# Attention values and output projections dealt as one step per PSUM bank, with one bias addition per bank of values

## The reference

```python
x = x + _L0_xattn_ref(_layernorm(x), ctx_512, ...)
x = x + _L0_ffn_ref(_layernorm(x), ...)
x = x + _L1_xattn_ref(_layernorm(x), ctx_512, ctx_512, ...)
x = x + _L1_ffn_ref(_layernorm(x), ...)
...
# layer 0 attention: causal self-attention plus attention to the context
v = _heads(x @ Wv + bv)
y = jnp.einsum('bhqk,bhkd->bhqd', jax.nn.softmax(att, axis=-1), v)
...
vc = _heads(cross_input @ Wcv + bcv)
y = y + jnp.einsum('bhqk,bhkd->bhqd', jax.nn.softmax(attc, axis=-1), vc)
return y.transpose(0, 2, 1, 3).reshape(x.shape[0], T, C) @ Wp + bp
```

## Time and profile before

| | us |
|---|---|
| median of three runs | 2109.8 |
| lowest and highest run | 2107.66, 2111.73 |
| the profiled execution, its time | 2102.05 |
| its span in the trace | 2100.2 |
| TensorE busy | 1729.6 (82%) |
| VectorE busy | 1344.1 (64%) |
| ScalarE busy | 1165.2 (55%) |
| GpSimd busy | 740.4 (35%) |
| mean granted clock of TensorE | 0.912 |

### The profile page before, as it was taken

One profiled execution on the slowest core, in us unless ns is written; L12 is line 12 of the kernel. 1 busy time (PEld: TensorE's weight loads), 2 busy tenths in 40 slices (PEclk: granted clock), 3 DMA queues, 4 the chain that ended last, 5 costly groups with the idle time before them and its releaser, 6 DMA issues.

```text
span 2100.2 us, 34206 instructions
## 1 busy us (share of the span) xinstructions
PE 1729.6 (82%) x10016; PEld 745.4 (35%) x10016; DVE 1344.1 (64%) x2478; ACT 1165.2 (55%) x2178; POOL 740.4 (35%) x984
## 2 busy tenths in 40 slices
PE   5676688898889879997889778987989888777776
PEld 1233234432344324433443234422443244232224
DVE  6454575667656575767566665757576766717378
ACT  1353347555855566554855575555755485571586
POOL 3303323632254325431353324431453223241034
PEclk7788889999999989998999989998999999986988
DMA  7213321323132312322132313231142213005023
GB/s 193 66 51 91 93 74 35 106 69 101 38 89 78 89 51 62 102 77 77 42 107 72 103 31 87 77 98 51 44 104 68 80 47 87 21 16 166 22 80 101
DMA packets 106991, 159.96 MB, mean 76 GB/s; under 512 B 20656, under 2 KB 83248, under 8 KB 106800
## 3 DMA queue, kind: packets, MB, share of 16 engines
q1 hardware_dynamic: 101904, 156.43, 26.8%
q10 hardware_dynamic: 4896, 1.18, 0.3%
HBM read 105.00 MB, written 51.38 MB: 74 GB/s over the span
## 4 chain that ended last, share of the span: by engine, by line
PE 49%; DVE 14%; POOL 13%; issue 11%; ACT 8%; DMA 4%; SPq 2%; ACTq 0%; POOLq 0%; DVEq 0%
PE acc L1375 11%; PE mx L1340 11%; PE st L1361 9%; DVE nmax L1161 6%; PE misc L1315 4%; PE misc L1287 4%; POOL qk L810 3%; PE misc L1327 3%; PE misc L1402 3%; POOL parts L812 2%; POOL parts L808 2%; PE misc L1429 2%; POOL parts L814 2%; ACT probs L918 1%; DMA hid<-in_L_ffn_w_dram 1%
## 5 line engine op out<-in xcount | busy, mean ns | idle before, releaser
L1161 DVE TENSOR_REDUCE nmax<-mx 128x1 f32<-128x512 f32 (+2 forms) x1376 | 877.9, 673 | 471.2 <-PE mx L1340 280.3
L918 ACT ACTIVATE probs<-st 128x512 f32<-128x512 f32 (+3 forms) x1536 | 772.0, 549 | 592.2 <-PE st L1361 393.9
L1340 PE MATMUL mx<-stack 96*128 96x512 bf16 (+3 forms) x1536 | 570.5, 383 | 189.7 <-DVE nmax L1161 136.0
L1361 PE MATMUL st<-stack 99*128 99x512 bf16 (+3 forms) x1536 | 566.0, 377 | 63.4 <-ACT probs L918 51.7
L1340 PEld LDWEIGHTS mx<-stack 96*128 96x128 bf16 x1536 | 154.0, 100 | 414.2 <-DVE nmax L1161 307.4
L1361 PEld LDWEIGHTS st<-stack 99*128 99x128 bf16 x1536 | 151.4, 100 | 414.1 <-ACT probs L918 250.2
L808 POOL TENSOR_TENSOR parts<-qk,zero 128x512 bf16<-128x512 f32 x94 | 98.2, 1045 | 304.5 <-ACT qk L901 304.5
L820 POOL TENSOR_TENSOR nparts<-nmax,zero 128x16 bf16<-128x16 f32 x96 | 20.7, 215 | 398.9 <-DVE nmax L1161 392.2
L1375 PE MATMUL acc<-probs,v_x 128*32 128x512 f32 x1024 | 154.3, 678 | 0.0
L1375 PE MATMUL acc<-probs,v_f 128*32 128x512 f32 x1024 | 142.2, 629 | 0.4 <-ACT probs L918 0.3
L1364 PE MATMUL st<-mask_st,identb 128*128 128x128 bf16 x512 | 112.5, 222 | 0.0
(11 more groups left out here) (235 smaller groups left out, 2044.0 us busy)
## 6 DMA issues: line engine op xcount, KB each, us to landing
parts_xk<-parts SPq DMA_DIRECT2D x48, 128.0 KB
parts_xq<-parts SPq DMA_DIRECT2D x48, 128.0 KB
stack<-parts_xq SPq DMA_DIRECT2D x32, 192.0 KB, 3.2
stack<-parts_xk SPq DMA_DIRECT2D x32, 192.0 KB, 3.6
...
```

Source lines behind the costliest of these rows:

```text
L918: act.activation(probs[:, j % P_SLOTS, c, T - w:], st_bank(n, 4 * j + c)[:, 0:w], ACT.Exp, scale=SCALE).then_inc(exp_done, 1)
L1161: dve.tensor_reduce(nmax[:, ring, first:first + NT * (len(cs) - 1) + 1:NT], src, AX.X, ALU.max, negate=True).then_inc(mx_free, 1)
L1340: last = pe.matmul(o, stack[0:ROWS, r, 0, c, P * i:P * i + P], stack[0:ROWS, r, 1, c, 0:w], start=True, stop=not causal)
L1361: last = pe.matmul(o[:, 0:w], stack[0:AUG, r, 1, c, P * j:P * j + P], stack[0:AUG, r, 0, c, T - w:T], start=True, stop=not causal)
```

## The change

`v` and `residual` become two steps each, with an index h of the bank, and the hand-written lists give each half its own entry, followed by an empty place. VectorE adds the bias of a whole bank of values in one 128x512 instruction (before, two of 128x256). The semaphore `v_done` goes: `values` waits for the reads of both `misc` banks. In the last turn's ends, where no slots are (`AFTER`), the halves follow each other directly. The waits of `stats` and of the tail's loads name the halves; nothing else is changed there.

```diff
--- before.py
+++ after.py
@@ -169,12 +169,16 @@
             [("stack", u) for u in us[2 * m:3][:2]]]
 
 
+def values_of(b, p):
+    return [("v", b, p, 0), None, ("v", b, p, 1), None]
+
+
 def project(b, p):
-    return [("v", b, p), None] + project_qk(b, p)
+    return values_of(b, p) + project_qk(b, p)
 
 
 def layer0_end(b):
-    return [("mid_bias", b), ("y_T", b, "A"), None, None, ("residual", b, "A"), None]
+    return [("mid_bias", b), ("y_T", b, "A"), None, None, ("residual", b, "A", 0), None, ("residual", b, "A", 1), None]
 
 
 def layer0_ffn(b):
@@ -196,7 +200,7 @@
 
 
 def layer1_end(b):
-    return [("y_T", b, "C"), None, ("residual", b, "C"), None, ("stats", b, "E"), None, None, ("norm", b, "E"),
+    return [("y_T", b, "C"), None, ("residual", b, "C", 0), None, ("residual", b, "C", 1), None, ("stats", b, "E"), None, None, ("norm", b, "E"),
             ("finish", b), None, None]
 
 
@@ -211,11 +215,11 @@
     if b == 0:
         return [("load0", 1)] + slots(us[:1], project(0, "s"), 1, True) + slots(us[1:3], weights([0, 1]), 1) + \
             slots(us[3:4], tokens0(1), 1) + slots(us[4:5], project_qk(1, "x"), 1) + \
-            slots(us[5:8], [("v", 1, "x"), ("load_mid", 0)] + weights([2, 3]) + project_qk(1, "s"), 1)
+            slots(us[5:8], values_of(1, "x") + [("load_mid", 0)] + weights([2, 3]) + project_qk(1, "s"), 1)
     more = b + 1 < B
     loads = [("load1", b - 1)] + ([("load0", b + 1)] if more else [])
     if b == 1:
-        start = slots(us[:1], [None] * 6 + layer0_end(0) + [("v", 1, "s")], 2) + \
+        start = slots(us[:1], [None] * 6 + layer0_end(0) + values_of(1, "s"), 2) + \
             slots(us[1:5], layer0_ffn(0) + layer1_start(0), 2)
     else:
         start = slots(us[:5], [None] * 6 + layer1_end(b - 2) + layer0_ffn(b - 1) + layer1_start(b - 1), b + more)
@@ -232,9 +236,9 @@
 
 
 FIRST = turn_units(0)
-BEFORE = [("load0", 0), ("consts_load", 0)] + tokens0(0) + [("consts", 0)] + first_qk(0, "x", FIRST) + [("v", 0, "x")] + \
+BEFORE = [("load0", 0), ("consts_load", 0)] + tokens0(0) + [("consts", 0)] + first_qk(0, "x", FIRST) + values_of(0, "x") + \
     warm_up(FIRST)[3:] + [("consts_rest", 0)]
-AFTER = close((B - 2, "f", NU - 1)) + warm_up(turn_units(B))[:3] + layer1_end(B - 2) + [("v", B - 1, "f")] + \
+AFTER = close((B - 2, "f", NU - 1)) + warm_up(turn_units(B))[:3] + layer1_end(B - 2) + values_of(B - 1, "f") + \
     warm_up(turn_units(B))[3:] + slots(turn_units(B), [], B, True) + close((B - 1, "f", NU - 1)) + layer1_end(B - 1)
 
 TURNS = [[s for s in steps if s] for steps in
@@ -242,8 +246,8 @@
 
 
 RING_USES = {
-    "misc": {"weights": 1, "ctx_T": 1, "norm_T": 2, "project": 1, "v": 2, "negmax_T": 1, "heads_out": 1,
-             "y_T": 2, "residual": 2, "quant_T": 2, "hidden": 1, "down_T": 1, "down": 1},
+    "misc": {"weights": 1, "ctx_T": 1, "norm_T": 2, "project": 1, "v": 1, "negmax_T": 1, "heads_out": 1,
+             "y_T": 2, "residual": 1, "quant_T": 2, "hidden": 1, "down_T": 1, "down": 1},
     "parts": {"project": 1},
 }
 
...
@@ -1139,15 +1142,13 @@
                                          ALU.add).then_inc(misc_free[slot], 1)
 
             def v(s):
-                p = s.args[0]
-                bias = Bv[p + "v"][:, :].rearrange("p (h d) -> p h d", d=D)
-                for k in range(2):
-                    wait_misc_full(dve, s, k)
-                    slot = misc_slot(s, k)
-                    for t in range(2):
-                        dve.tensor_tensor(v_aug[p][:, 2 * k + t, :, 0:D],
-                                          misc[slot][:, C * t:C * t + C].rearrange("p (h d) -> p h d", d=D), bias,
-                                          ALU.add).then_inc(*((v_done[p], 1) if t == 0 else (misc_free[slot], 1)))
+                p, h = s.args
+                bias = Bv[p + "v"][:, :].rearrange("p (h d) -> p h d", d=D).unsqueeze(1).to_broadcast([P, 2, H, D])
+                wait_misc_full(dve, s)
+                slot = misc_slot(s)
+                dve.tensor_tensor(v_aug[p][:, 2 * h:2 * h + 2, :, 0:D],
+                                  misc[slot].rearrange("p (t h d) -> p t h d", t=2, d=D), bias,
+                                  ALU.add).then_inc(misc_free[slot], 1)
 
             def maxima(s):
 
@@ -1178,14 +1179,13 @@
                                   ALU.mult).then_inc(misc_free[slot], 1)
 
             def residual(s):
-                k = s.args[0]
+                k, h = s.args
                 x_ = xmid if k == "A" else x1_of(s)
                 dve.wait_ge(biased[k], s.b.at(1))
-                for h in range(2):
-                    slot = misc_slot(s, h)
-                    wait_misc_full(dve, s, h)
-                    dve.tensor_tensor(x_[:, 2 * h:2 * h + 2, :], misc[slot][:, :].rearrange("p (t c) -> p t c", c=C),
-                                      x_[:, 2 * h:2 * h + 2, :], ALU.add).then_inc(misc_free[slot], 1)
+                slot = misc_slot(s)
+                wait_misc_full(dve, s)
+                dve.tensor_tensor(x_[:, 2 * h:2 * h + 2, :], misc[slot][:, :].rearrange("p (t c) -> p t c", c=C),
+                                  x_[:, 2 * h:2 * h + 2, :], ALU.add).then_inc(misc_free[slot], 1)
 
             def finish(s):
 
@@ -1317,16 +1317,16 @@
                 last.then_inc(misc_full, 1)
 
             def v(s):
-                w = s.args[0] + "v"
+                p, h = s.args
+                w = p + "v"
                 (src, reads), ks = turned(s, w), W[w].shape[1]
-                for h in range(2):
-                    wait_misc(pe, s, h, reads)
-                    for t in range(2):
-                        first = P * (2 * h + t)
-                        for k in range(ks):
-                            last = pe.matmul(misc[misc_slot(s, h)][:, C * t:C * t + C], src[:, k, first:first + P],
-                                             W[w][:, k, :], start=k == 0, stop=k == ks - 1)
-                    last.then_inc(misc_full, 1)
+                wait_misc(pe, s, 0, reads)
+                for t in range(2):
+                    first = P * (2 * h + t)
+                    for k in range(ks):
+                        last = pe.matmul(misc[misc_slot(s)][:, C * t:C * t + C], src[:, k, first:first + P],
+                                         W[w][:, k, :], start=k == 0, stop=k == ks - 1)
+                last.then_inc(misc_full, 1)
 
             def maxima(s):
                 k, n, r = s.args[0], s.mx(), s.n.slot(STACKS)
@@ -1368,7 +1368,8 @@
                 j, n, (_, p, g) = s.args[0], s.n, s.unit
                 w = T - P * j if p == "s" else T
                 if j == 0:
-                    pe.wait_ge(v_done[p], s.b.times(2, 2).at())
+                    for h in range(2):
+                        wait_misc_read(pe, s, 0, ("v", s.unit[0], p, h))
                     pe.wait_ge(heads_full, n.at(1))
                 pe.wait_ge(exp_done, n.times(16, 4 * j + 4 + ST_BANKS).at())
                 for c in range(HU):
@@ -1392,16 +1393,15 @@
                     turn_tiles(s, m, [y_[:, t, P * m:P * m + P] for t in range(NT)], ident, reads=reads)
 
             def residual(s):
-                k = s.args[0]
+                k, h = s.args
                 reads = [misc_read(s, m, ("y_T", s.key[1], k)) for m in range(KC)]
-                for h in range(2):
-                    wait_misc(pe, s, h, reads)
-                    for t in range(2):
-                        first = P * (2 * h + t)
-                        for m in range(KC):
-                            last = pe.matmul(misc[misc_slot(s, h)][:, C * t:C * t + C], yT[:, m, first:first + P],
-                                             W[k + "o"][:, m, :], start=m == 0, stop=m == KC - 1)
-                    last.then_inc(misc_full, 1)
+                wait_misc(pe, s, 0, reads)
+                for t in range(2):
+                    first = P * (2 * h + t)
+                    for m in range(KC):
+                        last = pe.matmul(misc[misc_slot(s)][:, C * t:C * t + C], yT[:, m, first:first + P],
+                                         W[k + "o"][:, m, :], start=m == 0, stop=m == KC - 1)
+                last.then_inc(misc_full, 1)
 
             def quant_T(s):
                 pe.wait_ge(quant, s.b.times(5, 5).at())
```

9 lines of the change are left out of this document (4 added, 5 removed).

## The result

| | before | after |
|---|---|---|
| median, us | 2108.8 (4 runs, 2107.66 to 2111.73) | 2134.5 (4 runs, 2131.52 to 2136.08) |
| ratio to before | | 1.0125, 95% interval 1.0105 to 1.0145 |
| profiled execution, time and span | 2102.05, 2100.2 | 2133.04, 2131.2 |
| mean granted clock of TensorE | 0.912 | 0.896 |

The change is slower by 26 us. The waits of the page are of one kind with the earlier trace rows: VectorE holds TensorE's maxima up less than before (307.4 then), ScalarE's Exps wait for scores 10 us more (393.9 then), and the rest is spread. Their totals don't show where 26 us went.

A forecast was written before the change was run, and what follows sets the result against it. It took f0, f1 and x3 as bound by TensorE's own work, other units by waits. +3.0 us per turn gave +18.0 for turns 2 to 7; with turn 1 +1.6 and turn 0 -4.0, +15.6 on 2109.8: 2125 us, range 2096 to 2140.

The forecast's parts named there:

- the slide of cards: List of x0 to s0 grows from 103 to 107 entries over 80 slots, moving other steps: +2.35, +0.65, +0.5 us a turn.
- Splitting the bursts: Five bursts of `v` and residual per turn: splitting fills TensorE's waits, 0.1 us each, -0.5 per turn, bounds 0 and -2.75.
- The bias: VectorE's bias additions, one per bank: 0.06 us for each of 48 banks, 3 us beside TensorE-bound units, 0 on the path.
- x3: `down` in x3 comes one slot earlier, losing cover for ScalarE's copy: +2.35 us a turn, bounds 0 and 3.
- The Gelus: End of x1: Gelus follow one Exp more, table load and Gelus end 1.3 us later; +0.65 a turn, bounds 0 and 1.3.
- s0: First key projection of `f` moves from slot 68 to 69, its chain to `stack` starts later: +0.5 us, bounds 0 and 0.9.
- x0 and x1's start: Steps there move together by a slot and keep their spacing: 0, bounds -1 and +1.
- Turn 0: Third weight's wait met two slots later, -1.4 us; fourth weight's load leaves earlier, -2.6; together -4.0, bounds -4.5 and 0.
- Turn 1: Shorter lists grow more: `down` loses its slot (+2.35), projection a slot earlier (-0.5), two bursts in x0 (0.25 taken): +1.6 us.
- The bursts as bottleneck: Four-slot cycles around each burst: five splits win 0.55 us each, x3's 2.35 is not paid; 2095 us, chance 0.25.
- That the slide costs little: At the four `down`s only the waits themselves are paid, 0.8 us a turn; 2115.5 us, chance 0.15.
- That the clock falls in x3: Waits at each `down` put half of x3 at TensorE's lower clock, 3.3 us a turn; 2145 us, chance 0.10.

The follow-up runs named there:

- kernel 1: Kernel before with empty places after the undivided v and residual, so all lists are as long as in the changed kernel; 2133.5 us, 1.0103.
- Kernel 5: Changed kernel with the four `down`s of turns 2 to 7 back in the slots of before; 2109.0 us, 1.0022.
- kernel 6: Changed kernel with the Gelus of turns 2 to 7 one slot earlier again, ahead of the Exp of slot 33; 2123.4 us, 1.0074.
- kernel 4: Changed kernel with the list of x0 to s0 in turns 2 to 7 at its old length, turn 1's x1 to s0 list also shortened; 2097.3 us, 0.9949.
- bias only: Kernel before with both halves of v and of residual in one entry, lists unchanged, plus the 512-wide bias and values waiting for misc; 2109.8 us, 1.0007.
- experiment 9: Kernel before, v and residual undivided, with empty places making every list but that of x0 to s0 slide; 2096.0 us, 0.9961.
- Kernel 7: Kernel before with three empty places behind turn 0's undivided v, so the second layer's weights stand where the change has them; 2105.3 us, 0.9981.
- kernel 12: Kernel 4 with both halves of turn 0's v in one entry, so the second layer's weights stand where they did before; 2107.1 us, 0.9989.
- kernels 2: Changed kernel with the looped turns' lists cut back to old length, second halves taking the empty entries; turns 0 and 1 share one for v; 2114.3 us, 1.0017.

## Why the prediction was right, and where it was not

2125 was forecast with a range of 2096 to 2140, and slower by over 0.2% with 0.67; the time was 2134.5, inside the range, but half a us outside the forecast's own 2118 to 2134. Sign and mechanism held: the slide of cards that the diff doesn't name decides, and the split counts for nothing. The sum was 15.6 us and should have been 26.

By the profiles the 31 us between the two executions fall so, forecast in brackets: turn 0 -8.2, with what stands ahead of it -9.1 (-4.0); turn 1 +5.5 (+1.6); turns 2 to 6 +18.8 (+15.0); turn 7 +11.2 (+3.0); the tail +4.5 (0, and mostly chance). The loop's +3.8 a turn lies near the forecast's 3.0 partly by luck: x0 to x3 lost 7.4 together, where x1 to x3 had 3.0 and x0 nothing, and s2 and f2, which had no term, gave back 3.3. Turn 7 shows it. It has no next batch, so the change moves nothing in its s2 and its f1 to f3; s2 lost 0.8, f2 gained nothing, and the losses of x0 to x3 (8.9) stand nearly alone. Taking turn 7 like the other turns was the largest single miss of the sum.

*Splitting the bursts*, -0.5 a turn. The hand layout of f0 and f1 is what happened. In f0 `y_T` waits (0.43 by TensorE's row, 0.5 forecast), the halves of the residual take 1.89 us with the latency (1.75 forecast), and ScalarE idles 1.57 instead of 3.53 us, without any gain in length:

```profile
1122.74 1.09 PE L1287 MATMUL misc<-ident,y_s 128*128 128x128 f32 x8 [0.43 <-POOL y_s L834]
...
1126.08 1.89 PE L1402 MATMUL misc<-W,yT 128*128 128x256 f32 x8
...
1128.22 1.09 ACT L921 ACTIVATE probs<-st 128x512 f32<-128x512 f32 x2 [1.57 <-PE st L1361]
```

f0 +0.1, f1 -0.1: forecast 0. Even "the halves save 0.35, `y_T` gives it back" can be read off, from kernel 1's f0 (+0.5, undivided) against after's (+0.1). The 0.1 for each burst beyond these two was not found.

*The bias*, 0 on the path: right. VectorE's busy time fell by 2.5 us (1344.1 to 1341.6) against 3 worked out from the rows. By the fixed part of 120 cycles that the Trainium skill gives (VectorE: DVE Perf Modes, TRN2 errata) the estimate was 6; the runs side with the rows, and the time doesn't care.

*x3*, +2.35 (bounds 0 and 3). Kernel 5 puts `down`'s part at 2.0 to 2.6. The four waits grew by 2.55. The 3.3 by which the unit grew isn't that term alone, and my sign ("x3 2 us longer") was met by `norm_T` in part. Only two of the `down`s waited over 0.5, not three: the fourth had 0.49.

*The Gelus*, +0.65 (bounds 0 and 1.3): mis-sized, and outside its bounds. It is 2.1, 12.6 us over six turns where 3.9 stood. "Load and Gelus end 1.3 us later" (1.5 by kernel 6) left out the Square that moves into the gap between Gelus and table load; the order showed it, and its 1.2 us is most of the missing part.

*s0*, +0.5: right about the chain. From the first key bias to the end of TensorE's wait it took 29.30 us before and 29.45 after:

```profile
1056.32 0.69 ACT L904 ACTIVATE qk<-misc,b_fk 128x512 f32<-128x512 f32 x1 [0.58 <-PE misc L1315]
...
1085.77 0.39 PE L1340 MATMUL mx<-stack 96*128 96x512 bf16 x1 [2.06 <-DMA stack<-parts_fk]
```

Between s0's start and that end lay 36.46 us before and 35.33 after, 1.1 less, while the part of x3's growth that isn't `down`'s is 1.7: 0.6 in all, by this reckoning and in this turn. But my sign, a wait for `parts_fk` that is 0.5 longer, did not come: it is 2.06 against 2.75. "What lies between is hidden" overlooked TensorE's wait for GpSimd in s1, which grew by 1.0, and the lower level behind it; s1 lost 1.8, and the wait in s2 gave part of that back.

*x0 and x1's start*, 0 (bounds ±1). x0 grew by 1.3, but kernel 4, with the old list, has 0.8 of that, and bias only 0.9. Nothing can be told apart there.

*What had no term.* f2 gains 1.1 and s2 2.2 a turn. In f2 it is the wait of experiment 9. In s2, over turns 2 to 6, the wait for `stack` is 1.0 shorter (3.0 to 2.0 in the mean). From its end to the unit's end, where the clock stayed at 1.00 throughout, it took 15.5 us before (turns 3 and 6) and 14.6 in after and in every kernel with after's lists and the split there, and 14.7 in kernels 1 and 9, which slide without the split: 0.9 is the slide of `project(b+1, "x")`. The remaining 0.3 is the clock, which fell in s2 in three of the five turns before and in two after.

*Turn 0*, -4.0 (bounds -4.5 and 0): mis-sized, -9.3 in s1 to s3. Both mechanisms are there: VectorE's wait for the third weight fell from 16.22 to 14.34 us (under 15.5, as forecast), and the queue sends the fourth weight's load at 210.04, 3.1 us earlier, as forecast.

```profile
196.87 2.29 DVE L1025 TENSOR_REDUCE wsum<-hid 128x1 f32<-128x2048 f32 x1 [14.34 <-DMA hid<-in_L_ffn_w_dram]
199.68 0.50 PE L1340 MATMUL mx<-stack 96*128 96x384 bf16 x1 [15.31 <-DVE nmax L1162]
...
204.95 1.26 SPq L668 DMA_DIRECT2D stack<-parts_xq  x3
206.25 1.35 SPq L668 DMA_DIRECT2D stack<-parts_xk  x3
...
210.04 0.43 SPq L614 DMA_DIRECT2D hid<-in_L_ffn_w_dram  x1
...
216.82 2.29 DVE L1025 TENSOR_REDUCE wsum<-hid 128x1 f32<-128x2048 f32 x1 [6.89 <-DMA hid<-in_L_ffn_w_dram]
...
219.76 0.61 PE L1340 MATMUL mx<-stack 96*128 96x512 bf16 x1 [7.74 <-DVE nmax L1162]
```

The same two waits of TensorE before:

```profile
199.00 0.50 PE L1340 MATMUL mx<-stack 96*128 96x384 bf16 x1 [17.30 <-DVE nmax L1161]
...
223.97 0.61 PE L1340 MATMUL mx<-stack 96*128 96x512 bf16 x1 [12.42 <-DVE nmax L1161]
```

They are 2.0 and 4.7 shorter, 6.7 together. I had counted the load's 3.1 for the fourth weight, and forgotten that its wait, too, is met two slots of work later. The granted clock of s2 rose as well, from 0.74 to 0.80 in windows over the unit; how the other 2.6 us divide between that and the rest stays open.

*Turn 1*, +1.6: it was +5.5 in the profiles. x3's +3.2 follows the loop. The miss is in x0, +3.8, for which I had taken a gain of 0.25: there `y_T` moved two slots earlier, from 10 to 8, and waits for GpSimd's sum. The row before:

```profile
267.59 1.48 PE L1287 MATMUL misc<-ident,y_s 128*128 128x128 f32 x8 [1.37 <-POOL y_s L831]
```

and after:

```profile
259.64 1.75 PE L1287 MATMUL misc<-ident,y_s 128*128 128x128 f32 x7 [3.75 <-POOL y_s L834]
```

I had seen this wait for f0, where the list loses one slot, and not carried it to turn 1, whose short list loses two. Kernel 7, with turn 0's slide and `y_T` in its old slot, waits 2.49 there, and kernel 12, with the old turn 0 and `y_T` in its new slot, 2.63: so about 1.1 of the 2.4 us is turn 0's gain taken back by the same sum on GpSimd, and 1.3 the two slots. The other 1.4 of x0's 3.8 is not explained; kernels 2 and 3, with the list of before, have this x0 at 21.4 and 21.5 where before had 23.1.

*The rivals.* The bursts as bottleneck fell with kernels 2 and 9. That the slide costs little fell with kernel 1. That the clock falls in x3 did not happen: it stayed at 1.00 with waits of 1.52 and 1.32 us. The Trainium skill (TensorE: Matmul & The Clock Gate, on oscillation) describes a kernel with longer waits between its stretches, so x3 doesn't speak against it; I had taken it without asking how long its waits were. But the rival was half right elsewhere: the clock fell longer where it fell before, in x1 with x2 (0.86 to 0.81 in turn 4), and it fell anew in s1 (1.00 to 0.89, 0.8 us in each turn of the loop), behind a wait of 2.42 us.
